# Output projection and layer norm of the first cross and first self attention in one block, the norm in two halves of tokens

## The chip, the cores and the metric

One core of one Trainium2 chip runs the whole kernel. Its engines are TensorE (PE; the load of its stationary operand is shown as PEld), VectorE (DVE), ScalarE (ACT), GpSimd (POOL) and SyncE (SP, which here issues the DMAs). Each has its own stream of instructions, and they meet only at semaphores. The metric is the device time of one launch in microseconds, before as the median of 3 runs.

## The reference, cut to what matters

A Perceiver of two layers. x is 512 rows (2 batches of 256) of 256 numbers in float32, the context 2 x 4096 rows of 256. `ln` is the layer norm without gain or bias.

```python
x = x + xattn0(ctx, ln(x), mask) @ Wo.T     # first cross attention, 16 heads of 16
x = x + sn(selfattn0(ln(x)), W_proj)        # first self attention, causal, spectral norm: a scale on the product
x = x + experts(ln(x))                      # 12 experts, the best 3 of each token, two layers and a GELU
x = x + xattn1(ln(x), ctx)                  # second cross attention, 16 heads of 64
x = x + selfattn1(ln(x)) @ Wo
x = x + quantised_ffn(ln(x))

def ln(x):
    m, v = mean(x, -1), var(x, -1)
    return (x - m) / sqrt(v + 1e-5)
```

The change concerns the ends of the first two lines (product with the output weights, addition into x) and the `ln` at the start of the second and the third.

## The kernel before, in words

The program is a row of blocks. A block holds one stream for each engine, written out by hand, with all waits between engines as counts on semaphores (`wait_ge`, `then_inc`). No scheduler moves anything. At the end of a block all engines meet before the next begins; in the trace such a border shows as a branch (L106, L1261, L1481, ...) and a stretch in which all of them idle.

x lies in SBUF as 4 tiles of 128 tokens (`NT` = 4), with 256 columns, which as the inner dimension of a product are 2 slices of 128 (`KT` = 2). PSUM has eight banks of 512 float32 columns: `banks[0:4]` are a_all and o_all, `s_banks` the four of s_all.

Place 1 lies between the first cross attention and the first self attention, place 2 between the first self attention and the experts. At both stand two blocks:

- `rows_project` (L1249). TensorE turns the attention's output with 8 transposes, slice by slice (L1282: all four tiles of slice 0 into one bank, then of slice 1). ScalarE copies each bank to `srcT` (L1297). TensorE waits for both copies and multiplies with the output weights, tile by tile, into one bank each (L1288). VectorE adds each tile into x as it comes ready, at place 1 by `add_to_x` (L1313), at place 2 with the spectral scale (L2379).
- `layer_norm` (L96). VectorE takes the statistics of four tiles (L115), aggregates them to mean and variance (L118) and adds epsilon (L120). GpSimd raises 128x4 numbers to the power -1/2 (L134). VectorE normalises four tiles into xn (L123). TensorE turns xn with 8 transposes (L146). VectorE copies slice 0 to xnT (L129), ScalarE slice 1 (L155).

Behind place 1 `self_attention` (L1441) begins. Its SyncE stream loads the weights of the experts, GpSimd splits the first half of them into two float16 parts (`halve`, L1793 and L1796) and only then turns to the causal selections (L1503) that the products with the values wait for. Behind place 2 `experts` (L1804) begins: two small products for the routing (L1846, L1850), then 144 matmuls for each layer (L1865), while VectorE compares and weighs.

`rows_project` and `layer_norm` are also used for the second cross and self attention, which the change leaves as they are.

Of the kernel before, what the change touches and what calls it, by code (L numbers as in the profile page):

```python
# [10 lines left out]
F32 = mybir.dt.float32  # L11
# [3 lines left out]
ALU = mybir.AluOpType  # L15
ACT = mybir.ActivationFunctionType
# [22 lines left out]
class Chip:  # L39


    def __init__(self, nc, ctx):
        self.nc, self.ctx, self.sems = nc, ctx, []
        self.sem_scope = ctx.enter_context(ExitStack())
        self.s_all = self.psum("s_all", 2048)
        self.s_ps = [self.s_all[:, 0:1024], self.s_all[:, 1024:2048]]
        self.s_banks = [self.s_all[:, i * 512:(i + 1) * 512] for i in range(4)]
        self.a_all, self.o_all = self.psum("a_all", 1024), self.psum("o_all", 1024)
        self.a_ps = [self.a_all[:, 0:512], self.a_all[:, 512:1024]]
        self.o_ps = [self.o_all[:, 0:512], self.o_all[:, 512:1024]]  # L50
        self.banks = [self.a_ps[0][:, :], self.a_ps[1][:, :], self.o_ps[0][:, :], self.o_ps[1][:, :],
                      *self.s_banks]
        self.x = self.sb("x", [P, NT, D], F32)
        self.xn = self.sb("xn", [P, NT, D], F32)
        self.xnT = self.sb("xnT", [P, KT, TOK], F32)
        self.ident = self.sb("ident", [P, P], F32)
        self.ones = self.sb("ones", [P, P], F32)
        self.half = self.sb("half", [P, 8], F32)
# [1187 lines left out]
                output((PAIRS - 1, W - 1))  # L1246


def rows_project(chip, tag, src, dims, weight, finish, bias_in=None, after=()):  # L1249


# [59 lines left out]
def add_to_x(chip):  # L1311
    def finish(dve, t, done):
        dve.tensor_tensor(chip.x[:, t, :], chip.banks[t][:, 0:D], chip.x[:, t, :], ALU.add).then_inc(done, 1)  # L1313
    return finish
# [1025 lines left out]
def perceiver(nc, t, out):  # L2340

    with ExitStack() as ctx:
# [17 lines left out]
        with ExitStack() as block0:  # L2360
            wo = Prefetch(chip, "o0", block0, t["a0o"])
            weights = [Prefetch(chip, f"s0{n}", block0, t[f"s0{n}"]) for n in "qkv"]
            with ExitStack() as scope:
                att = chip.sb("att0", [P, NT, D], F32, scope)
                with ExitStack() as inner:
                    buffers = SmallCrossBuffers(chip, "x0", inner, queries[0], *scratch[0])
                    cross_attention_small(chip, "x0", buffers, att, mask_out, t["ones2"], t["qrows"], t["fold"], after=[wo, *weights])
                rows_project(chip, "o0", att, D, wo, add_to_x(chip))


            layer_norm(chip, "ln1")
            with ExitStack() as scope:
                expert_weights = ExpertWeights(chip, scope, t["f0w1"], t["f0w2"], t["f0p"], t["f0u"], t["f0b"])
                att = chip.sb("att1", [P, NT, D], F32, scope)
                wo = Prefetch(chip, "o1", scope, t["s0p"])
                self_attention(chip, "s0", weights, att, [expert_weights, wo], scale=sc[:, 0:1], mask=t["causal"])

                def finish(dve, n, done):
                    dve.scalar_tensor_tensor(out=chip.x[:, n, :], in0=chip.banks[n][:, 0:D], scalar=sc[:, 1:2],  # L2379
                                             in1=chip.x[:, n, :], op0=ALU.mult, op1=ALU.add).then_inc(done, 1)  # L2380
                rows_project(chip, "o1", att, D, wo, finish)


                layer_norm(chip, "ln2")
                experts(chip, "moe", expert_weights)
        chip.recycle_semaphores()

# [96 lines left out]
```

## Time and profile before

| | |
|---|---|
| median of 3 runs | 1714.96 us |
| lowest, highest | 1714.06, 1715.53 us |
| the profiled execution | 1716.51 us |
| its span, first to last instruction | 1714.8 us |
| mean granted TensorE clock in it | 0.946 of full |
| busy TensorE, VectorE, ScalarE, GpSimd | 91%, 65%, 52%, 40% |

The profile is one execution. In its rows a name such as `o_srcT<-s_all` is the output, then the inputs; numbers in names are left out, so that `ln_st` is the tile of each layer norm and `o_pw` the weights of each output projection. `128x256 f32` are partitions and elements in each. A row of the timeline that has x4 holds four instructions merged, from the start of the first to the end of the last. The bracket at its end is the idle time of the engine before it and what ended that. PEclk is the granted TensorE clock as a share of 2.4 GHz: 1.00 is 2.4 GHz, 0.50 is 1.2 GHz.

### The profile page before, as it was taken

What the parts mean: (1) busy time and instruction counts of PE and PEld (TensorE: products, weight loads), DVE (VectorE), ACT (ScalarE), POOL (GpSimd) and SP (SyncE); (2) the same over time, 40 slices, a digit from 0 to 9 for tenths busy, and PEclk for the clock granted to TensorE, in tenths of its full rate; (3) what the DMA queues carried; (4) which work ended last, traced back from release to release, by engine and by line L of the source; (5) the groups of instructions that cost most, each with busy time, mean ns of one, the idle gap of its engine ahead of it and who ended that gap; (6) DMA issues with size and microseconds to landing.
All of it is one profiled execution on the core that took longest, in us unless ns stands there. A gap on an engine that the chain in (4) does not pass through costs nothing. (4 is left out here: it accounts for less than half of the span.)

```text
span 1714.8 us, 42108 instructions
## 1 busy us (share of the span) xinstructions
PE 1555.2 (91%) x15980; PEld 879.7 (51%) x15980; DVE 1107.0 (65%) x1786; ACT 889.4 (52%) x1204; POOL 690.9 (40%) x536
## 2 busy tenths in 40 slices
PE   7999999999499999999778958999999999996774
PEld 3455454444133333433454426777777777772442
DVE  4656656665599999996327756666666666605446
ACT  5555555554078888887241015555555555532525
POOL 5320000000111111111143108999999999951800
PEclk9999999999589999999798979999999999998887
DMA  7987978887432222220400057555556545212000
GB/s 252 225 238 207 232 233 203 232 222 182 127 95 68 67 67 67 67 67 26 157 2 1 1 141 223 151 159 142 139 153 159 156 126 162 61 35 93 2 1 13
DMA packets 178223, 212.24 MB, mean 124 GB/s; under 512 B 57096, under 2 KB 151572, under 8 KB 173486
## 3 DMA queue, kind: packets, MB, share of 16 engines
q1 hardware_dynamic: 177520, 210.44, 44.9%
q8 instruction: 93, 1.52, 0.4%
q14 instruction: 34, 0.28, 0.1%
q10 hardware_dynamic: 576, 0.00, 0.0%
HBM read 122.78 MB, written 87.57 MB: 123 GB/s over the span
## 5 line engine op out<-in xcount | busy, mean ns | idle before, releaser
L1202 POOL TENSOR_TENSOR x_r<-x_p 128x1024 f16<-128x1024 f32 x256 | 479.0, 1893 | 24.3 <-ACT x_p L1178 17.2
L1217 DVE TENSOR_REDUCE x_mx<-a_all 128x2 f32<-128x1024 f32 x249 | 304.7, 1224 | 147.2 <-PE a_all L1101 147.2
L1178 ACT ACTIVATE x_p<-s_all 128x1024 f32<-128x1024 f32 x256 | 248.4, 1022 | 223.5 <-PE s_all L1084 223.5
L769 ACT ACTIVATE x_p<-s_all 128x1024 f32<-128x1024 f32 x256 | 261.5, 1024 | 60.8 <-PE s_all L676 55.4
L824 DVE TENSOR_REDUCE x_mx<-a_all 128x1 f32<-128x512 f32 x352 | 231.5, 681 | 21.7 <-PE o_all L687 12.9
L1084 PE MATMUL s_all<-x_q,x_k 64*128 64x256 f16 x3072 | 210.2, 269 | 0.0
L1119 PEld LDWEIGHTS o_all<-x_v,x_p 128*128 128x128 bf16 x2048 | 178.7, 97 | 40.1 <-issue 40.1
L1119 PE MATMUL o_all<-x_v,x_p 128*128 128x129 f16 x2048 | 197.3, 221 | 0.9 <-POOL x_r L1202 0.9
L1120 PE MATMUL o_all<-x_v,x_r 128*128 128x65 f16 x2048 | 192.5, 193 | 0.0
L1084 PEld LDWEIGHTS s_all<-x_q,x_k 64*128 64x128 f16 x3072 | 149.5, 94 | 62.0 <-issue 0.8
L1120 PEld LDWEIGHTS o_all<-x_v,x_r 128*128 128x128 f16 x2048 | 180.7, 98 | 0.0
L715 PE MATMUL o_all<-x_p,x_vf 128*32 128x256 f32 x2048 | 163.7, 393 | 3.1 <-ACT x_osb L758 2.7
L687 PE MATMUL a_all<-x_k,x_qa 64*128 64x512 f16 x352 | 113.3, 399 | 23.3 <-DMA x_v<-values 21.8
L798 POOL TENSOR_TENSOR x_mcol<-x_nm,x_zero 128x4 f16<-128x4 f32 x32 | 6.8, 213 | 298.7 <-DVE x_nm L831 298.7
L824 DVE TENSOR_REDUCE x_mx<-o_all 128x1 f32<-128x512 f32 x160 | 109.1, 682 | 6.6 <-PE a_all L687 2.4
L1101 PE MATMUL a_all<-x_k,x_q 64*128 64x512 f16 x498 | 97.2, 387 | 12.3 <-DVE x_mx L1217 7.3
L676 PE MATMUL s_all<-x_qb,x_k 64*128 64x256 f16 x1024 | 103.9, 278 | 0.0
L233 POOL TENSOR_TENSOR q_rs<-q_ve,half 128x4 f32<-128x4 f32 x1 | 1.0, 1021 | 247.0 <-DVE q_ve L246 247.0
L1078 PE MATMUL s_all<-x_qm,x_ones 64*128 64x512 f16 x512 | 100.0, 387 | 0.0
L495 DVE TENSOR_TENSOR vst<-a_all,vst 128x512 f16<-128x512 f32 (+1 forms) x96 | 57.8, 602 | 42.1 <-ACT vst L459 41.4
L495 DVE TENSOR_TENSOR vst<-o_all,vst 128x512 f16<-128x512 f32 (+1 forms) x96 | 57.7, 602 | 41.5 <-ACT vst L459 41.0
L459 ACT ACTIVATE vst<-a_all 128x512 f16<-128x512 f32 (+1 forms) x96 | 51.5, 536 | 52.7 <-PE a_all L422 52.2
(363 smaller groups left out, 2767.7 us busy)
## 6 DMA issues: line engine op xcount, KB each, us to landing
values<-vst SPq DMA_DIRECT2D x16, 2064.0 KB, 10.5
x_v<-values SPq DMA_DIRECT2D x32, 1032.0 KB, 5.3
keys<-kst SPq DMA_DIRECT2D x32, 1024.0 KB, 6.8
x_k<-keys SPq DMA_DIRECT2D x128, 256.0 KB, 5.3
x_k<-keys SPq DMA_DIRECT2D x192, 64.0 KB, 2.1
values<-vst SPq DMA_DIRECT2D x16, 528.0 KB, 11.6
x_v<-values SPq DMA_DIRECT2D x32, 264.0 KB, 2.7
cf<-in_ctxT SPq DMA_DIRECT2D x16, 512.0 KB, 9.9
```

The source lines that it names most:

```text
L495: dve.tensor_tensor(lo, src, hi, ALU.subtract).then_inc(lo_done, 1)
L676: last = pe.matmul(chip.s_ps[g % 2][:, c * SQ:(c + 1) * SQ], kbuf[w][r, (2 * g + j) * P:(2 * g + j + 1) * P], qb[w][r, :], start=True, sto ...
L687: pe.matmul(bank(place)[:], qa[w][r, qt * P:(qt + 1) * P], kbuf[w][r, c * 512:(c + 1) * 512], start=True, stop=True).then_inc(chunk_ready, 1)
L715: last = pe.matmul(o[32 * c:32 * c + 32, 0:SQ], vf[w][:, kt, :], prob[g % NP][:, c, :], start=(g == 0), stop=(g == GR - 1), skip_group_che ...
L769: act.activation(prob[g % NP][:], chip.s_ps[g % 2][:].rearrange("p (c q) -> p c q", q=SQ), ACT.Exp, scale=hd ** -0.5).then_inc(p_ready, 1)
L824: dve.tensor_reduce(mx[a[1] % 2][:, n // 8, n % 8:n % 8 + 1], bank(place)[:], AX.X, ALU.max).then_inc(chunk_done, 1)
L1084: last = pe.matmul(s[:, c * SQ:(c + 1) * SQ], k[w][kp][r, (2 * g + j) * P:(2 * g + j + 1) * P], q[w][qp][r, :], start=False, stop=(kp == 1 ...
L1119: pe.matmul(o[:, qt * VC:(qt + 1) * VC], hi, v[w][:, kt, :], start=begin, stop=False, skip_group_check=True)
L1120: last = pe.matmul(o[:, qt * VC:qt * VC + 1 + hd], rest[i][:, c, qs], v[w][:, kt, 0:1 + hd], start=False, stop=end, skip_group_check=True)
L1178: act.activation(prob[g % NP][:], chip.s_ps[g % 2][:].rearrange("p (c q) -> p c q", q=SQ), ACT.Exp, scale=hd ** -0.5).then_inc(p_ready, 1)
L1202: pool.tensor_tensor(rest[g % NP][:], prob[g % NP][:], hi, ALU.subtract).then_inc(rest_done, 1)
L1217: dve.tensor_reduce(mx[a[1] % 2][:, n // 4, 2 * (n % 4):2 * (n % 4) + 2], chunk_banks(u, g)[:, :].rearrange("p (h c) -> p h c", h=2), AX.X ...
```

## The change

At both places the two blocks become one, `project_and_norm`, and `layer_norm` is no longer called there. The transposes of the attention's output are ordered by halves of tokens, tiles 0 and 1 in one bank and tiles 2 and 3 in the other, and the product of a tile waits only for the copy of its half. VectorE takes the statistics of a tile directly behind its addition; a class `HalfNorm` then does variance, power, normalisation, transposes and copy for tiles 0 and 1 and for tiles 2 and 3. The transposes of xn go to `s_banks[2:4]`, and ScalarE copies both halves.

```diff
--- before.py
+++ after.py
@@ -1244,6 +1244,106 @@
 
                 all_units(body)
                 output((PAIRS - 1, W - 1))
+
+class HalfNorm:
+
+    def __init__(self, chip, tag, scope, banks):
+        self.chip, self.banks = chip, banks
+        self.st = chip.sb(f"{tag}_st", [P, NT, 6], F32, scope)
+        self.mv = chip.sb(f"{tag}_mv", [P, NT, 2], F32, scope)
+        self.ve = chip.sb(f"{tag}_ve", [P, NT], F32, scope)
+        self.rs = chip.sb(f"{tag}_rs", [P, NT], F32, scope)
+        (self.stats, self.spread, self.var, self.rstd, self.normed, self.turned, self.copied) = (
+            chip.sem(f"{tag}_{n}") for n in ("stats", "aggr", "var", "rstd", "xn", "tr", "trout"))
+
+    def stats_of(self, dve, t, src):
+        dve.bn_stats(self.st[:, t, :], src).then_inc(self.stats, 1)
+
+    def variance(self, dve, h):
+        dve.wait_ge(self.stats, 2 * h + 2)
+        for t in (2 * h, 2 * h + 1):
+            dve.bn_aggr(self.mv[:, t, :], self.st[:, t, :]).then_inc(self.spread, 1)
+        dve.wait_ge(self.spread, 2 * h + 2)
+        hs = slice(2 * h, 2 * h + 2)
+        dve.tensor_scalar(self.ve[:, hs], self.mv[:, hs, 1], 1e-5, None, ALU.add).then_inc(self.var, 1)
+
+    def power(self, pool, h):
+        hs = slice(2 * h, 2 * h + 2)
+        pool.wait_ge(self.var, h + 1)
+        pool.tensor_tensor(self.rs[:, hs], self.ve[:, hs], self.chip.half[:, hs], ALU.pow).then_inc(self.rstd, 1)
+
+    def apply(self, dve, t, out, src):
+        dve.wait_ge(self.rstd, t // 2 + 1)
+        dve.tensor_scalar(out, src, self.mv[:, t, 0:1], self.rs[:, t:t + 1], ALU.subtract, ALU.mult).then_inc(self.normed, 1)
+
+    def turn(self, pe, h):
+        pe.wait_ge(self.normed, 2 * h + 2)
+        for k in range(KT):
+            for t in range(2):
+                last = pe.transpose(self.banks[h][:, (2 * k + t) * P:(2 * k + t + 1) * P],
+                                    self.chip.xn[:, 2 * h + t, k * P:(k + 1) * P], self.chip.ident[:])
+        last.then_inc(self.turned, 1)
+
+    def copy(self, act, h):
+        act.wait_ge(self.turned, h + 1)
+        act.activation(self.chip.xnT[:, :, h * 2 * P:(h + 1) * 2 * P], self.banks[h].rearrange("p (k t) -> p k t", k=KT),
+                       ACT.Copy).then_inc(self.copied, 1)
+
+def project_and_norm(chip, tag, src, weight, finish):
+
+    nc = chip.nc
+    with ExitStack() as scope:
+        w = weight.w
+        srcT = chip.sb(f"{tag}_srcT", [P, KT, TOK], F32, scope)
+        norm = HalfNorm(chip, f"{tag}_ln", scope, chip.s_banks[2:4])
+        tr, tr_out, ready, done = (chip.sem(f"{tag}_{n}") for n in ("tr", "trout", "rdy", "done"))
+        with nc.Block() as block:
+            @block.gpsimd
+            def _(pool):
+                for h in range(2):
+                    norm.power(pool, h)
+
+            @block.tensor
+            def _(pe):
+                for h in range(2):
+                    for k in range(KT):
+                        for t in range(2):
+                            last = pe.transpose(chip.s_banks[h][:, (2 * k + t) * P:(2 * k + t + 1) * P],
+                                                src[:, 2 * h + t, k * P:(k + 1) * P], chip.ident[:])
+                    last.then_inc(tr, 1)
+                pe.wait_ge(weight.loaded, 16)
+                for t in range(NT):
+                    pe.wait_ge(tr_out, t // 2 + 1)
+                    for k in range(KT):
+                        last = pe.matmul(chip.banks[t][:, 0:D], srcT[:, k, t * P:(t + 1) * P], w[:, k, :],
+                                         start=(k == 0), stop=(k == KT - 1))
+                    last.then_inc(ready, 1)
+                for h in range(2):
+                    norm.turn(pe, h)
+
+            @block.scalar
+            def _(act):
+                for h in range(2):
+                    act.wait_ge(tr, h + 1)
+                    act.activation(srcT[:, :, h * 2 * P:(h + 1) * 2 * P], chip.s_banks[h].rearrange("p (k t) -> p k t", k=KT),
+                                   ACT.Copy).then_inc(tr_out, 1)
+                for h in range(2):
+                    norm.copy(act, h)
+
+            @block.vector
+            def _(dve):
+                for h in range(2):
+                    for t in (2 * h, 2 * h + 1):
+                        dve.wait_ge(ready, t + 1)
+                        finish(dve, t, done)
+                        dve.wait_ge(done, t + 1)
+                        norm.stats_of(dve, t, chip.x[:, t, :])
+                    norm.variance(dve, h)
+                for t in range(NT):
+                    norm.apply(dve, t, chip.xn[:, t, :], chip.x[:, t, :])
 
 def rows_project(chip, tag, src, dims, weight, finish, bias_in=None, after=()):
@@ -2365,10 +2465,8 @@
                 with ExitStack() as inner:
                     buffers = SmallCrossBuffers(chip, "x0", inner, queries[0], *scratch[0])
                     cross_attention_small(chip, "x0", buffers, att, mask_out, t["ones2"], t["qrows"], t["fold"], after=[wo, *weights])
-                rows_project(chip, "o0", att, D, wo, add_to_x(chip))
-
-
-            layer_norm(chip, "ln1")
+                project_and_norm(chip, "o0", att, wo, add_to_x(chip))
+
             with ExitStack() as scope:
                 expert_weights = ExpertWeights(chip, scope, t["f0w1"], t["f0w2"], t["f0p"], t["f0u"], t["f0b"])
                 att = chip.sb("att1", [P, NT, D], F32, scope)
@@ -2378,10 +2476,7 @@
                 def finish(dve, n, done):
                     dve.scalar_tensor_tensor(out=chip.x[:, n, :], in0=chip.banks[n][:, 0:D], scalar=sc[:, 1:2],
                                              in1=chip.x[:, n, :], op0=ALU.mult, op1=ALU.add).then_inc(done, 1)
-                rows_project(chip, "o1", att, D, wo, finish)
-
-
-                layer_norm(chip, "ln2")
+                project_and_norm(chip, "o1", att, wo, finish)
                 experts(chip, "moe", expert_weights)
         chip.recycle_semaphores()
```

VectorE's stream at place 1, from the last branch ahead of it to the first behind it; `o0` is this projection, `ln1` the norm behind it. Before:

```order
L1303 UNCONDITIONAL_BRANCH
L1313 TENSOR_TENSOR x<-a_all,x 128x256 x2
L1313 TENSOR_TENSOR x<-o_all,x 128x256 x2
L1261 UNCONDITIONAL_BRANCH
L112 UNCONDITIONAL_BRANCH
L115 BN_STATS ln1_st<-x 128x6 x4
L118 BN_AGGR ln1_mv<-ln1_st 128x2 x4
L120 TENSOR_SCALAR ln1_ve<-ln1_mv 128x4
L123 TENSOR_SCALAR xn<-x,ln1_mv,ln1_rs 128x256 x4
L129 COPY xnT<-a_all 128x512
L106 UNCONDITIONAL_BRANCH
```

And of the changed kernel:

```order
L1336 UNCONDITIONAL_BRANCH
L1413 TENSOR_TENSOR x<-a_all,x 128x256
L1262 BN_STATS o0_ln_st<-x 128x6
L1413 TENSOR_TENSOR x<-a_all,x 128x256
L1262 BN_STATS o0_ln_st<-x 128x6
L1267 BN_AGGR o0_ln_mv<-o0_ln_st 128x2 x2
L1270 TENSOR_SCALAR o0_ln_ve<-o0_ln_mv 128x2
L1413 TENSOR_TENSOR x<-o_all,x 128x256
L1262 BN_STATS o0_ln_st<-x 128x6
L1413 TENSOR_TENSOR x<-o_all,x 128x256
L1262 BN_STATS o0_ln_st<-x 128x6
L1267 BN_AGGR o0_ln_mv<-o0_ln_st 128x2 x2
L1270 TENSOR_SCALAR o0_ln_ve<-o0_ln_mv 128x2
L1279 TENSOR_SCALAR xn<-x,o0_ln_mv,o0_ln_rs 128x256 x4
L1303 UNCONDITIONAL_BRANCH
```

The statistics have moved in between the additions, variances and epsilon come once for each two tiles, all normalisations still stand in a row behind the second variance, and the copy to xnT is gone.

TensorE's stream at place 1, `att0` being the attention's output. Before:

```order
L1276 UNCONDITIONAL_BRANCH
L1282 MATMUL s_all<-ident,att0 128x128 x8
L1288 MATMUL a_all<-o0_pw,o0_srcT 128x256 x4
L1288 MATMUL o_all<-o0_pw,o0_srcT 128x256 x4
L1261 UNCONDITIONAL_BRANCH
L139 UNCONDITIONAL_BRANCH
L146 MATMUL a_all<-ident,xn 128x128 x8
L106 UNCONDITIONAL_BRANCH
```

And of the changed kernel:

```order
L1309 UNCONDITIONAL_BRANCH
L1314 MATMUL s_all<-ident,att0 128x128 x8
L1321 MATMUL a_all<-o0_pw,o0_srcT 128x256 x4
L1321 MATMUL o_all<-o0_pw,o0_srcT 128x256 x4
L1285 MATMUL s_all<-ident,xn 128x128 x8
L1303 UNCONDITIONAL_BRANCH
```

The transposes of xn follow the products without a branch, into s_all. The place 2 has the same rows with `o1`, `att1` and `ln2`.

## Rows read from the trace of the kernel before

**Rows 1.** Timeline, place 1: start, duration, engine, line, operation, tiles, count, [idle before].
```profile
815.37 1.38 PE L1282 MATMUL s_all<-ident,att 128*128 128x128 f32 x8 [0.97 <-PEq L649]
816.04 0.60 ACT L1297 ACTIVATE o_srcT<-s_all 128x512 f32<-128x512 f32 x1 [2.38 <-PE s_all L1282]
816.79 0.60 ACT L1297 ACTIVATE o_srcT<-s_all 128x512 f32<-128x512 f32 x1 [0.15 <-PE s_all L1282]
...
819.61 0.42 DVE L1313 TENSOR_TENSOR x<-a_all,x 128x256 f32<-128x256 f32 x1 [4.78 <-PE a_all L1288]
...
823.00 0.42 DVE L1313 TENSOR_TENSOR x<-o_all,x 128x256 f32<-128x256 f32 x1 [1.26 <-PE o_all L1288]
823.87 0.42 DVE L1313 TENSOR_TENSOR x<-o_all,x 128x256 f32<-128x256 f32 x1 [0.44 <-PE o_all L1288]
824.82 1.40 DVE L115 BATCH_NORM_STATS2 ln_st<-x 128x6 f32<-128x256 f32 x4 [0.53 <-PEq L1261]
826.25 0.38 DVE L118 BATCH_NORM_AGGREGATE ln_mv<-ln_st 128x2 f32<-128x6 f32 x4
826.67 0.17 DVE L120 TENSOR_SCALAR ln_ve<-ln_mv 128x4 f32<-128x4 f32 x1
826.92 1.02 POOL L134 TENSOR_TENSOR ln_rs<-ln_ve,half 128x4 f32<-128x4 f32 x1 [26.70 <-DVE ln_ve L120]
827.97 1.38 DVE L123 TENSOR_SCALAR xn<-x,ln_mv,ln_rs 128x256 f32<-128x256 f32 x4 [1.13 <-POOL ln_rs L134]
...
829.41 1.97 PE L146 MATMUL a_all<-ident,xn 128*128 128x128 f32 x8 [5.58 <-DVE xn L123]
830.56 0.69 DVE L129 COPY xnT<-a_all 128x512 f32<-128x512 f32 x1 [1.21 <-PE a_all L146]
831.41 0.60 ACT L155 ACTIVATE xnT<-a_all 128x512 f32<-128x512 f32 x1 [14.03 <-PE a_all L146]
```

**Rows 2.** Timeline, place 2.
```profile
893.64 1.08 ACT L1297 ACTIVATE o_srcT<-s_all 128x512 f32<-128x512 f32 x2 [2.54 <-PE s_all L1282]
...
896.01 0.48 DVE L2379 SCALAR_TENSOR_TENSOR x<-a_all,sn,x 128x256 f32<-128x256 f32 x1 [3.57 <-PE a_all L1288]
...
898.60 0.48 DVE L2379 SCALAR_TENSOR_TENSOR x<-o_all,sn,x 128x256 f32<-128x256 f32 x1 [0.38 <-PE o_all L1288]
...
906.20 0.60 ACT L155 ACTIVATE xnT<-a_all 128x512 f32<-128x512 f32 x1 [11.47 <-PE a_all L146]
```

**Rows 3.** Groups by line and form, 811 to 834: busy us, mean ns of one.
```profile
L115 DVE BATCH_NORM_STATS2 ln_st<-x 128x6 f32<-128x256 f32 x4 | 1.4, 414 | 0.5 <-PEq L1261 0.5
L123 DVE TENSOR_SCALAR xn<-x,ln_mv,ln_rs 128x256 f32<-128x256 f32 x4 | 1.4, 407 | 1.1 <-POOL ln_rs L134 1.1
```

**Rows 4.** Stretches: length, busy PE, PEld, DVE, ACT, POOL, PEclk, DMA, GB/s.
```profile
816.00:822.80 6.80, 6.02 (x18) 4.58 (x16) 0.85 (x2) 1.19 (x2) 0.00 (x0) 0.50 0.00 0
826.20:839.80 13.60, 7.20 (x14) 3.52 (x15) 3.63 (x15) 1.40 (x3) 2.58 (x3) 0.50 0.47 165
901.20:918.30 17.10, 12.48 (x32) 5.90 (x33) 8.57 (x44) 2.66 (x5) 1.01 (x1) 0.50 0.00 1
```

**Rows 5.** Timeline, GpSimd's first selection in the first self attention.
```profile
869.34 1.24 POOL L1503 TENSOR_SCALAR_AFFINE_SELECT s_p<-s_p 128x512 f32<-128x512 f32 x2 [0.32 <-ACT s_p L1702]
```

**Rows 6.** The page's groups: a small tensor-tensor of GpSimd.
```profile
L798 POOL TENSOR_TENSOR x_mcol<-x_nm,x_zero 128x4 f16<-128x4 f32 x32 | 6.8, 213 | 298.7 <-DVE x_nm L831 298.7
```

**Rows 7.** Timeline, VectorE's casts and GpSimd's memset behind place 1.
```profile
832.28 0.52 POOL L1494 MEMSET s_nm<- 128x512 f16 x1 [4.34 <-POOLq L106]
...
832.32 0.56 DVE L1709 CAST s_ident<-ident 128x128 f16<-128x128 f32 x1 [1.07 <-PEq L106]
...
834.06 0.23 DVE L1713 CAST s_mkb<-ident 128x128 bf16<-128x128 f32 x1 [1.11 <-DMA s_mk<-in_causal]
```

**Rows 8.** Timeline, expert matmuls at both clocks.
```profile
917.95 0.60 PE L1865 MATMUL s_all<-ewh,moe_xl 128*128 128x512 f16 x1
...
918.38 0.39 PE L1865 MATMUL s_all<-ewh,moe_xh 128*128 128x512 f16 x1
```

## The prediction

> **What bounds the kernel now.** I read four views, in this order. The busy shares of the whole span (the table of the section on the profile) have TensorE at 91%. That says nothing of the two places the change touches, because there the engines work one after another. The timeline of the first place [rows 1] shows it as a chain: each instruction starts when one on another engine ends. Follow it down: transposes, a ScalarE copy, projection matmuls, VectorE's adds, the statistics, GpSimd's power, VectorE's normalisation, transposes, a copy. No other work of the program lies beside it, so whatever is taken out of this chain comes off the time. The second place [rows 2] is the same chain at the doubled clock. The table of stretches [rows 4] then shows at which clock TensorE ran there, and the timeline of the stage behind [rows 5] what could swallow a gain.
>
> Call E the end of the last of the four adds into x. At place 1, E is 823.87 + 0.42 = 824.29, and the last copy into xnT ends at 831.41 + 0.60 = 832.01: 7.72 us [rows 1]. At place 2, E is 898.60 + 0.48 = 899.08 and the copy ends at 906.20 + 0.60 = 906.80: again 7.72 us [rows 2]. The two blocks together are all that the change edits.
>
> **From E to the end of the norm, per place** [rows 1, 3].
> - The block border. Before, the statistics start at 824.82, 0.53 after E. Now a wait on the same engine stands there; the nearest row is from the end of the statistics (826.22) to the aggregation (826.25), 0.03. Gain 0.50.
> - Statistics. Four in 1.40 before. Now three are done while TensorE projects, and one, 0.41 [rows 3], stands behind E. Gain 0.99.
> - Aggregation: two of four behind E, half of 0.38. Gain 0.19. The addition of epsilon stays (0.17).
> - The power on GpSimd. Its input has two columns where it had four. No row shows that. It costs at most the 1.02 of four columns; the cheapest tensor-tensor of GpSimd with this shape, another operation, takes 0.21 [rows 6]. I take 1.02, the row of the same operation. If it is 0.21, the normalisations of half 0 (0.73) hide it, and 0.45 more is gained at each place.
> - Normalisation. Half 0 is normalised while GpSimd works on half 1. On VectorE's stream, variance(1) stands ahead of apply(0), so half 0 isn't early; it only fills the wait. Behind the power two of four are left: 0.41 + 0.32 = 0.73 in place of 1.38 (0.32 is the step from one to the next, (1.38 - 0.41)/3). Gain 0.65.
> - Transposes and copy. Before, ScalarE's copy waited for all eight, 829.41 to 831.41, 2.00. Now half 1 has four; the row for four at this clock is the start of VectorE's copy, 830.56 - 829.41 = 1.15. Gain 0.85. The copy is ScalarE's in both (0.60); of the split form I know no row, so 0.60 to the 0.69 of VectorE's copy. VectorE's copy, now ScalarE's, lay beside the transposes before, and copy(0) lies there now: 0.
>
> Sum: 0.50 + 0.99 + 0.19 + 0.65 + 0.85 = 3.18 us per place, 6.36 for two.
>
> **Ahead of E.** The projection of tiles 0 and 1 no longer waits for the second ScalarE copy, only for the first.
> - Place 1: the copies start at 816.04 and 816.79, so matmuls start 0.75 earlier, soon after 816.64. TensorE is free by then, give or take a tenth: its transposes end at 816.75. VectorE keeps up, since at the low clock a tile comes each 1.7 us (from the first add to the third, 3.39 for two) and its add, its statistics and two waits take 0.9. Tile 2's add moves from 823.00 to 822.25. Tile 3 ran mostly behind the rise of the clock at 822.8 [rows 4], and this rise I leave where it is. From tile 2's add on, 0.55 us at the low clock does what 0.275 does at the high one, and of the 0.87 that a tile takes at the high clock (823.00 to 823.87) 0.595 is left behind 822.80: tile 3's add starts at 823.40. So E moves from 824.29 to 823.82: gain 0.47, bounds 0 and 0.75.
> - Place 2: one copy is 0.54 [rows 2], so tile 0's add starts at 895.47. But tiles come every 0.86 (four adds, 896.01 to 898.60) and VectorE now needs 0.48 + 0.03 + 0.41 = 0.92 for each, plus 0.42 for aggregation and epsilon of half 0. From 895.47: three rounds of 0.92 and 0.42 give 898.65, the fourth add ends at 899.13, against 899.08. Gain 0; bounds 0 and 0.54. What hid the statistics at place 1, the slow matmuls, isn't there.
>
> Total 6.36 + 0.47 + 0 = 6.83 us.
>
> **What it meets behind.** The loads of the expert weights are issued in the self-attention block behind place 1, and GpSimd splits them ahead of its first selection. They move with the start of that block, so the 3.65 us of place 1 are not lost to them. GpSimd has only 0.32 us of idle time before that selection [rows 5], though: a further gain on TensorE there (a clock that rises sooner) would run into GpSimd. Behind place 2 the expert block starts on xnT and everything in it is issued relative to that. All else of the program, before and behind, keeps its instructions.
>
> The profiled execution took 1716.51, 1.55 above the median of the runs, 1714.96; its span was 1714.8. 1716.51 - 6.83 = 1709.7 for such an execution, and for the median 1714.96 - 6.83 = 1708.1.
>
> **A rule that speaks against it.** The new overlap, normalisation of half 0 on VectorE beside the power on GpSimd, is one that before never had: GpSimd idled during all of VectorE's part and the reverse [rows 1]. In this kernel VectorE and GpSimd can disturb each other. A cast of 128x128 takes 0.56 beside GpSimd's memset and 0.23 alone [rows 7]. The Trainium skill, SBUF — State Buffer, "Who interferes with whom", says why: the two engines share a pair of ports that one instruction holds whole, when VectorE's runs in a two-port mode, and it lists copy, cast and tensor_scalar among those that can. The normalisation is a tensor_scalar. For it speaks only its kind; against it, that it takes 0.41 for 256 elements [rows 3] where the undisturbed cast takes 0.23 for 128, nearly in proportion, so no mode shows as faster than the other. That doesn't decide it.
>
> **Rivals.**
> 1. Port. One of the two waits for the other. If power(1) waits for both normalisations, it starts 0.73 - 0.05 = 0.68 later; if they wait for it, four stand behind it again, 0.65. Either way 0.7 per place: 6.83 - 1.4 = 5.4, time 1709.5. Chance 0.08.
> 2. The clock holds. TensorE's granted clock is at 1.2 GHz (0.50 of full) from 826.2 to 839.8 and from 901.2 to 918.3 [rows 4]; both falls come in the idle stretch between last projection and first transposes of xn (5.6 us at place 1 [rows 1]). The change cuts that stretch to about 2 us, with transposes of half 0 in it. If the clock stayed up, the eight transposes save about 0.5 per place (four took 815.37 to 816.04, 0.67, at the high clock and 1.15 at the low one), 1.0 in all. In the expert block at most half of TensorE's 12.48 busy us goes, 6.2; but VectorE's routing and first weighings lie in the same stretch, 8.57 us busy, and TensorE may be only four tiles ahead of them, so I take 4 of the 6.2. At place 1 rows 5 let little through, about 1. Together 6.83 + 1.0 + 4 + 1 = 12.8, time about 1702. Against it: even the split stretch is over half idle. The Trainium skill, TensorE: Matmul & The Clock Gate, "The HAM clock gate", says that the low clock is the default that activity lifts; by that too a shorter idle stretch is the better one, but rows give no bound. Chance 0.12, mostly for a part of it.
> 3. No change that can be told. What the borders and waits cost comes back: the power of half 1 queued behind, added waits, a rise of the clock that comes later. It needs 3.4 of the 6.83 lost. Chance 0.06.
> 4. Slower. The mechanism is a clock that stays low for long behind place 2: expert matmuls start every 0.43 at 1.2 GHz [rows 8] and so every 0.215 at 2.4. To lose 6.83 and 3.43 more, 10.3/0.215 = 48 further matmuls must run low; with all 144 of the first layer low it is 31 us at most, and the time at most 1708.1 + 31 = 1739. Against it: before, the rise came at 918.3 once they were issued without a gap. Chance 0.03.
>
> **How the numbers follow.** The forecast as summed has 0.71. Its own spread: power and transposes up to 0.9 each on the good side, the clock's rise in the next block about 1 us either way, copies and waits 0.5 on the bad one: 1705.3 to 1710. With the port and part of the clock's luck the range is 1705 to 1711. A measurement of this kernel can tell about 0.2%, 3.4 us, from no change; that is a time of 1711.5. Faster: 0.71 + 0.12 + 0.08 = 0.91, less 0.01 for mixed mishaps: 0.90. Same 0.07, slower 0.03.
>
> **What would show it.** From E to the end of the last xnT copy: 4.5 us at both places, for 7.72. The last add of place 2 no earlier than before, of place 1 about half a us earlier, counted from the first transpose. A two-column power near 1.0. Normalisations 0 and 1 beside the power, at 0.41 each; longer ones, or a power that starts late, would be the port. GpSimd's first selection at the same distance from the start of the self-attention block. The forecast is wrong if these hold and the total doesn't move, or if the granted clock's low stretches differ by several us.

## The result, and the profile after

Six runs of each kernel on one chip: 1709.20 us (1706.46 to 1710.82) for 1714.51 (1713.23 to 1717.57). The ratio is 0.9966, 95% interval 0.9953 to 0.9979: 3.6 to 8.1 us off, forecast 6.8. Later I measured the changed kernel twice more, each time beside before on one chip: 0.9938 (0.9925 to 0.9950) and 0.9949 (0.9930 to 0.9967). The three ratios are worth 5.8, 10.6 and 8.8 us; the first was the smallest, and I estimate the true gain at 8 to 10 us. That the kernel is faster is shown by all three. Its size is less certain: the intervals of the first and the second comparison don't overlap, and no run shows why.

The profiled execution took 1710.64, with a span of 1708.9. Place 1 in its timeline; columns as in [rows 1], which these rows answer.

```profile
818.28 1.06 PE L1314 MATMUL s_all<-ident,att 128*128 128x128 f32 x8 [0.97 <-PEq L649]
818.94 1.09 ACT L1331 ACTIVATE o_srcT<-s_all 128x512 f32<-128x512 f32 x2 [2.39 <-PE s_all L1314]
...
819.68 1.96 PE L1321 MATMUL a_all<-o_pw,o_srcT 128*128 128x256 f32 x8 [0.34 <-ACT o_srcT L1331]
820.83 0.42 DVE L1413 TENSOR_TENSOR x<-a_all,x 128x256 f32<-128x256 f32 x1 [3.09 <-PE a_all L1321]
...
821.28 0.43 DVE L1262 BATCH_NORM_STATS2 o_ln_st<-x 128x6 f32<-128x256 f32 x1
...
823.76 0.41 DVE L1413 TENSOR_TENSOR x<-o_all,x 128x256 f32<-128x256 f32 x1
824.21 0.43 DVE L1262 BATCH_NORM_STATS2 o_ln_st<-x 128x6 f32<-128x256 f32 x1
824.67 0.25 DVE L1267 BATCH_NORM_AGGREGATE o_ln_mv<-o_ln_st 128x2 f32<-128x6 f32 x2
824.95 0.17 DVE L1270 TENSOR_SCALAR o_ln_ve<-o_ln_mv 128x2 f32<-128x2 f32 x1
825.03 0.73 DVE L1279 TENSOR_SCALAR xn<-x,o_ln_mv,o_ln_rs 128x256 f32<-128x256 f32 x2
825.20 0.79 POOL L1275 TENSOR_TENSOR o_ln_rs<-o_ln_ve,half 128x2 f32<-128x2 f32 x1 [1.35 <-DVE o_ln_ve L1270]
...
825.81 0.66 PE L1285 MATMUL s_all<-ident,xn 128*128 128x128 f32 x4 [2.43 <-DVE xn L1279]
826.02 0.73 DVE L1279 TENSOR_SCALAR xn<-x,o_ln_mv,o_ln_rs 128x256 f32<-128x256 f32 x2 [0.27 <-POOL o_ln_rs L1275]
...
826.82 0.88 PE L1285 MATMUL s_all<-ident,xn 128*128 128x128 f32 x4 [0.35 <-DVE xn L1279]
827.73 0.60 ACT L1291 ACTIVATE xnT<-s_all 128x512 f32<-128x512 f32 x1 [0.63 <-PE s_all L1285]
```

E is 823.76 + 0.41 = 824.17, the last copy ends at 828.33: 4.16 us for 7.72. One statistics instruction stands behind E where four stood, and the second pair of normalisations starts 0.03 behind the power. Place 2, for [rows 2]:

```profile
895.89 0.47 DVE L2477 SCALAR_TENSOR_TENSOR x<-o_all,sn,x 128x256 f32<-128x256 f32 x1
...
900.16 0.60 ACT L1291 ACTIVATE xnT<-s_all 128x512 f32<-128x512 f32 x1 [0.87 <-PE s_all L1285]
```

4.40 us, again for 7.72. The stretches by clock, for [rows 4]: length, busy time of PE, PEld, DVE, ACT, POOL, granted clock, DMA share, GB/s.

```profile
816.00:820.00 4.00, 2.09 (x18) 1.70 (x15) 0.36 (x2) 1.44 (x3) 0.00 (x0) 1.00 0.00 0
820.00:827.10 7.10, 4.32 (x23) 3.34 (x22) 5.39 (x18) 0.62 (x2) 1.50 (x2) 1.00 0.01 2
827.10:837.40 10.30, 6.28 (x12) 2.49 (x11) 0.72 (x4) 1.40 (x4) 1.45 (x2) 0.50 0.75 282
898.80:912.40 13.60, 11.77 (x29) 5.11 (x30) 6.40 (x35) 3.15 (x6) 0.00 (x0) 0.50 0.00 0
```

Call the front the time from the last write of the first attention's output to E. At place 1 the clock is now at 2.4 GHz through all products. In before it fell at 816.0, and the front took 9.46 us; here it took 6.43. Against that stands a loss: behind xnT the first projection waits longer.

The table cuts all fourteen profiles at the same points, from their timelines. Its rows are named after the experiments of the next section. A: last write of the first attention's output. E: end of the last addition into x. C: end of the last copy to xnT. P: first projection of the self attention. B: last write of its output. L: first product of the experts. "Fall" is when the granted clock fell between A and E, counted from A, and "low" is how long it then stayed at 1.2 GHz.

```
us              A-E1  fall  low   E1-C1  C1-P   P-B    B-E2  E2-C2  C2-L  L-end
before          9.46  +1.2  6.8   7.72   2.56   57.87  6.64  7.72   0.30  807.67
before again    8.27  +2.8  3.4   7.73   2.65   57.62  6.64  7.71   0.31  807.29
after           6.43  none    -   4.16   3.39   58.02  6.62  4.40   0.30  807.85
after again     6.44  none    -   3.93   3.18   56.85  6.61  4.40   0.30  806.55
after third     6.44  none    -   3.93   3.23   56.72  6.62  3.94   0.31  806.89
place 1 only    6.44  none    -   3.93   2.94   56.91  6.64  7.73   0.30  806.62
place 2 only    8.27  +2.7  3.4   7.74   2.61   57.55  6.61  4.40   0.30  807.23
held            7.67  +0.8  3.4   4.78   2.94   58.17  6.62  5.14   0.31  807.17
merged whole    7.39  +1.2  3.4   7.46   2.96   57.16  6.16  7.45   0.30  807.81
early products  6.09  none    -   7.74   2.61   57.00  6.16  7.71   0.31  807.16
late products   9.45  +1.2  6.8   4.40   4.28   57.05  7.11  3.94   0.30  806.72
spare block     8.53  +2.5  3.4   3.94   2.56   57.58  6.62  4.39   0.31  807.25
mask early      6.44  none    -   3.93   1.42   57.77  6.62  4.39   0.30  807.43
loads early     7.66  +0.6  3.4   3.94   1.42   57.62  6.62  4.40   0.30  807.23
```

A itself lies between 814.2 and 817.9 in them, in code that is the same in all. This scatter of nearly 4 us is larger than most terms of the sum, which is why what follows goes by segments and not by times.

### The profile page after: what moved, and what is told of

The parts are those of the page before. It is cut to its first block and busy times, and to the rows that moved or that the text cites. A ratio compares the mean times of both kernels' runs of the same rounds, so it can differ in the third digit from the quotient of the medians.

```text
span 1708.9 us, 42088 instructions
## 1 busy us (share of the span) xinstructions
PE 1553.2 (91%) x15980; PEld 877.4 (51%) x15980; DVE 1106.8 (65%) x1786; ACT 891.3 (52%) x1206; POOL 692.9 (41%) x538
## 5 line engine op out<-in xcount | busy, mean ns | idle before, releaser
L1202 POOL TENSOR_TENSOR x_r<-x_p 128x1024 f16<-128x1024 f32 x256 | 479.3, 1895 | 23.9 <-ACT x_p L1178 17.1
```

What stands on the lines that cost most here:

```text
L1202: pool.tensor_tensor(rest[g % NP][:], prob[g % NP][:], hi, ALU.subtract).then_inc(rest_done, 1)
```

## The experiments

**The kernel before, again**, unedited.

> The kernel before, once more, for a second profile. Segments between fixed points of the timeline: from the end of the first cross attention (last write of att) to E (last addition into x) 9.46 us in the first profile, E to the end of xnT 7.72, from there to the first projection of the self attention 2.56, place 2: 6.64, 7.72, 0.30. Theory (fixed lengths, only TensorE's clock differs between executions): 7.72 and 7.72 again within 0.2; the 9.46 is 6.6 where the clock is at 2.4 GHz there, 9.5 where it falls to 1.2 as in the first profile. Rival (before always has the low clock at place 1, and the change lifts it): 9.46 again.

1717.82 us, one run. E to C is 7.73 and 7.71: these lengths repeat. The front was 8.27, with the clock falling at 820.7:

```profile
818.41 1.06 PE L1282 MATMUL s_all<-ident,att 128*128 128x128 f32 x8 [0.97 <-PEq L649]
819.08 1.08 ACT L1297 ACTIVATE o_srcT<-s_all 128x512 f32<-128x512 f32 x2 [2.38 <-PE s_all L1282]
...
820.30 3.36 PE L1288 MATMUL a_all<-o_pw,o_srcT 128*128 128x256 f32 x8 [0.83 <-ACT o_srcT L1297]
```

TensorE stood idle for 0.83 us ahead of the products, and 0.4 us after they began the clock fell; most of them ran at 1.2 GHz (the row has 3.36 us where after has 1.96).

**The changed kernel, again**, unedited.

> The changed kernel once more, with a profile and five rounds. First profile: end of attention to E 6.43, E to xnT 4.16 at place 1 and 4.40 at place 2, xnT to the first projection 3.39 (the causal mask landed 2.6 us after its issue; 1.8 in before). Theory of the sum: E to xnT 4.1 to 4.6 at both places, time 5 to 8 us under before, ratio about 0.9960. Rival clock: 6.43 is luck, in this profile it can be 9.0 (low clock). Rival mask: the earlier block makes the mask land late every time, 3.4 again; if it is scatter of the transfer, 2.6 to 3.4.

Ratio 0.9938 (0.9925 to 0.9950). Front 6.44 and no fall, for the second time. The causal mask, which the first projection waits for, was late again (C1-P 3.18). Luck alone became less likely for either.

**Place 1 only**

```diff
-                project_and_norm(chip, "o1", att, wo, finish)
+                rows_project(chip, "o1", att, D, wo, finish)
+                layer_norm(chip, "ln2")
```

> The change at place 1 only (output projection of the first cross attention and the norm behind it); place 2 as before. Theory of the sum: 3.2 us from E to xnT, 0 to 0.75 ahead of E by clock, so 3.2 to 3.9 us under before; place 2 at 6.64 + 7.72. Rival (the gain of place 1 is taken back by the wait for the mask or by GpSimd's split of the expert weights in the block behind): under 2.5 us, with the segment from xnT to the end of the self attention longer by the difference.

Ratio 0.9968 (0.9956 to 0.9980), 3.4 to 7.5 us off. E to C 3.79 less than before, and the front again without a fall. The gain isn't taken back.

**Place 2 only**, the same edit at place 1.

> The change at place 2 only (output projection of the first self attention and the norm behind it); place 1 as before. Theory of the sum: 3.2 to 3.4 us under before, all of it between E and xnT (7.72 to 4.4), nothing ahead of E (6.6 in both). Rival (the low clock of the expert block grows by what the norm shrinks): under 2 us, with a longer segment behind xnT.

Ratio 0.9975 (0.9965 to 0.9986), 2.4 to 6.0 us off. All of it lies in E2-C2, 4.40 for 7.72; the front at place 2 is 6.61 for 6.64. The low clock in the experts took nothing back: L-end is 807.23 for 807.67 and 807.29.

**Held normalisations**

```diff
+                dve.wait_ge(norm.rstd, 2)
                 for t in range(NT):
                     norm.apply(dve, t, chip.xn[:, t, :], chip.x[:, t, :])
```

> The changed kernel, but all four normalisations of a place wait for the power of half 1. It takes away the overlap of VectorE's normalisation with GpSimd's power. Theory of the sum: E to xnT grows by 0.65 to 0.75 at each place, from about 4.0 and 4.4 to 4.7 and 5.1; the second power stays at 0.8 or falls to 0.70. Rival port (the two engines block one another in the changed kernel): nearly no growth, since two normalisations beside the power would cost what four behind it do, and the second power falls clearly.

Ratio 0.9949 (0.9929 to 0.9968). E1-C1 is 4.78, against 3.93 to 4.16, and E2-C2 grew from 4.40 to 5.14, by 0.74. Its rows at place 2:

```profile
897.19 0.70 POOL L1275 TENSOR_TENSOR o_ln_rs<-o_ln_ve,half 128x2 f32<-128x2 f32 x1 [1.47 <-DVE o_ln_ve L1270]
897.93 1.38 DVE L1279 TENSOR_SCALAR xn<-x,o_ln_mv,o_ln_rs 128x256 f32<-128x256 f32 x4 [0.81 <-POOL o_ln_rs L1275]
```

The normalisations end 3.14 behind E where after has 2.59: the overlap is worth 0.55, which is the 0.65 of the sum less the 0.1 by which the power is slower beside it. The other 0.19 lies behind them: here all eight transposes stand there in a row, while in after those of half 0 are out of the way by then. So 0.74 comes near to 0.65 by two deviations that cancel in part.

The second power takes 0.70 alone and 0.79 to 0.80 beside the two normalisations (0.79 in the rows of after), in all profiles that have this overlap. So the two engines do disturb each other, by 0.1 us. The normalisation keeps its 0.41. The rival as I stated it, one waiting for the other's whole work, is refuted.

**Merged, norm whole**: the block of after, and behind E the stream of before.

```diff
-                    for t in (2 * h, 2 * h + 1):
-                        ...
-                        norm.stats_of(dve, t, chip.x[:, t, :])
-                    norm.variance(dve, h)
+                for t in range(NT):
+                    dve.wait_ge(ready, t + 1)
+                    finish(dve, t, done)
+                dve.wait_ge(done, NT)
+                for t in range(NT):
+                    norm.stats_of(dve, t, chip.x[:, t, :])
+                ...    # aggregation, epsilon, power, normalisation, transposes, copies as in layer_norm
```

> The changed kernel with early products and one block, but behind E the norm is done whole as before: four statistics, four aggregations, one power of four columns, four normalisations, eight transposes, two copies. Only the block border is gone. Theory of the sum: E to xnT 7.72 - 0.50 = 7.2 at both places; 3 us each above the changed kernel. Rival (the merged block itself is most of the gain): below 6.5.

Ratio 0.9985 (0.9973 to 0.9996). E to C is 7.46 and 7.45, not 7.2.

```profile
821.67 0.42 DVE L1423 TENSOR_TENSOR x<-o_all,x 128x256 f32<-128x256 f32 x1 [0.44 <-PE o_all L1321]
822.13 1.41 DVE L1262 BATCH_NORM_STATS2 o_ln_st<-x 128x6 f32<-128x256 f32 x4
823.57 0.38 DVE L1349 BATCH_NORM_AGGREGATE o_ln_mv<-o_ln_st 128x2 f32<-128x6 f32 x4
824.05 0.17 DVE L1351 TENSOR_SCALAR o_ln_ve<-o_ln_mv 128x4 f32<-128x4 f32 x1
824.37 1.02 POOL L1307 TENSOR_TENSOR o_ln_rs<-o_ln_ve,half 128x4 f32<-128x4 f32 x1 [24.29 <-DVE o_ln_ve L1351]
825.50 1.38 DVE L1279 TENSOR_SCALAR xn<-x,o_ln_mv,o_ln_rs 128x256 f32<-128x256 f32 x4 [1.28 <-POOL o_ln_rs L1307]
```

The border's term is as summed: 0.04 from E (822.09) to the statistics for 0.53 in before. Three hand-overs behind it are 0.06 to 0.08 longer each than in [rows 1], to epsilon 0.10, to the power 0.15, back 0.11. What makes them longer in this kernel stays open. Merging alone is a small part of the gain; the halves are the larger.

**Early products**: the two blocks of before, with the order of the transposes and the waits of the products as in after.

```diff
+                if split:    # the tags "o0" and "o1"
+                    ...      # transposes: tiles 0 and 1, then 2 and 3, one bank each
                 for t in range(NT):
+                    if split:
+                        pe.wait_ge(tr_out, t // 2 + 1)
```

> The kernel before with only the transposes of the attention's output ordered by halves and the products of a half released by its own copy, both blocks kept. As predicted: end of attention to E 0.47 shorter at a low clock; place 2 6.64 - 0.54 = 6.1 (no statistics in VectorE's way). Theory clock (the shorter gap between transposes and products at place 1, 0.3 for 0.8 us, keeps TensorE at 2.4 GHz): 6.0 at place 1 with a granted clock of 1.00 up to the last product, where the three profiles without early products had 8.3 to 9.5 and those with them 6.4. Rival luck (the clock's fall there has nothing to do with the order): 7.5 or more.

Ratio 0.9982 (0.9970 to 0.9995). Front 6.09, clock at 1.00 from 814.0 to 824.4:

```profile
814.00:824.40 10.40, 5.12 (x28) 4.07 (x27) 4.02 (x15) 1.08 (x2) 0.87 (x1) 1.00 0.00 0
```

At place 2 the front is 6.16 for 6.64, 0.48 shorter, where the sum has 0.54 for one copy.

**Late products**

```diff
+                pe.wait_ge(tr_out, 2)
                 for t in range(NT):
-                    pe.wait_ge(tr_out, t // 2 + 1)
```

> The changed kernel with the products waiting for both copies again. Theory clock: the clock falls at place 1 between transposes and products as in before, end of attention to E 8.3 to 9.5, time 2 to 3 us above the changed kernel. Theory of the sum as predicted: 0.5 to 0.75 more at place 1, and at place 2 about 0.3 to 0.5 more. Rival luck: 6.4 + 0.5 = 6.9 to 7.2 at a clock of 1.00.

Ratio 0.9957 (0.9945 to 0.9970). Front 9.45, and place 2 7.11 for 6.62. The fall came at +1.2, ahead of the first product in either version, so the order of the products didn't cause it. Merged whole, with early products, has its fall at +1.2 too, and the two differ in what follows. Late products, the low stretch and the products of tiles 0 and 1:

```profile
815.40:822.20 6.80, 6.02 (x17) 4.57 (x16) 2.12 (x7) 1.19 (x2) 0.10 (x1) 0.50 0.00 0
816.86 3.75 PE L1321 MATMUL a_all<-o_pw,o_srcT 128*128 128x256 f32 x8 [0.78 <-ACT o_srcT L1331]
```

And merged whole:

```profile
815.86:819.25 3.39, 3.35 (x11) 2.54 (x9) 0.42 (x1) 1.19 (x2) 0.00 (x0) 0.50 0.02 5
819.30:826.00 6.70, 2.33 (x11) 1.72 (x9) 3.73 (x14) 0.00 (x0) 1.02 (x1) 1.00 0.00 0
816.65 3.26 PE L1321 MATMUL a_all<-o_pw,o_srcT 128*128 128x256 f32 x8
```

With late products TensorE idled for 0.78 us ahead of them and the clock stayed low for 6.8 us; with early ones no idle time is shown there, and it rose after 3.4. The fronts are 9.45 and 7.39. Merged whole has no statistics between its additions, which is worth 0.34 without a fall (6.43 for 6.09); held and loads early have them, fell at +0.8 and +0.6, rose after 3.4 us as well, and took 7.67 and 7.66. Before stands with late products: +1.2, 6.8, 9.46. So the five profiles with an early fall divide by the order of the products.

The other falls divide nearly so. Products start at A + 1.9 with early products at the high clock, and at A + 2.4 (at the high clock) to 2.7 without. Falls at +0.6 to +1.2 are in both kinds (before, held, merged whole, late products, loads early), and when they come looks like luck. Falls at +2.5 to +2.8 are in three profiles, two without early products and the spare block, whose extra border moves its products to A + 2.4. In none of the nine others with early products did the clock fall after +1.2 ahead of E. With so few profiles that is likely rather than shown; the difference after an early fall rests on two profiles against three.

**Spare block** ahead of `project_and_norm` at place 1.

```diff
+                with chip.nc.Block() as block:
+                    @block.vector
+                    def _(dve):
+                        dve.tensor_copy(chip.ones[:, 0:1], chip.half[:, 0:1])
                 project_and_norm(chip, "o0", att, wo, add_to_x(chip))
```

> The changed kernel with a spare block (one copy of one column on VectorE) ahead of the projection of place 1. It moves all that follows in the program by one block, as the layer norm's block did in before. In the four profiles with two blocks a transfer of instructions of queue 14 lies 3 us ahead of the end of xnT and the mask lands 1.8 to 1.9 us after its issue; in the six with one block it lies 1.2 to 1.7 us behind it, right ahead of the mask's landing, at 2.2 us or more. Theory (the place of that instruction transfer delays the mask): if the spare block moves the transfer, first projection 2.6 us behind xnT again. Rival (the mask is late for another reason): 2.9 or more with the transfer elsewhere.

Ratio 0.9956 (0.9942 to 0.9970). C1-P fell to 2.56. In after, the mask's issue, VectorE's casts behind its landing, and the transfers by queue and kind from 829 to 832 (packets, MB, share of 16 engines) are:

```profile
828.59 0.36 SPq L1585 DMA_DIRECT2D s_mk<-in_causal  x1
...
831.21 0.23 DVE L1813 CAST s_mkb<-ident 128x128 bf16<-128x128 f32 x1 [2.21 <-DMA s_mk<-in_causal]
...
831.72 3.75 PE L1614 MATMUL o_all<-xnT,s0q_pw 128*128 128x512 f32 x4 [4.02 <-DVE s_mkb L1814]
```

```profile
q1 hardware_dynamic: 186, 0.58, 73.2%
q14 instruction: 1, 0.01, 0.7%
```

And with the spare block, from 830 to 833 (q14 had its transfer at 819.5):

```profile
830.19 0.36 SPq L1585 DMA_DIRECT2D s_mk<-in_causal  x1
...
831.98 0.23 DVE L1813 CAST s_mkb<-ident 128x128 bf16<-128x128 f32 x1 [1.11 <-DMA s_mk<-in_causal]
```

```profile
q1 hardware_dynamic: 168, 0.36, 52.8%
```

With the transfer of instructions out of the way the cast started 1.79 us behind the issue, with it 2.62 us. Twelve profiles load the mask in this block. In seven of them such a transfer comes 1.2 to 1.7 us behind C, and C1-P is 2.94 to 4.28. In the other five, the spare block's among them, it comes 2.9 us or more ahead of C, and C1-P is 2.56 to 2.65. That the transfer and the late mask go together is shown; through what it delays the mask is not.

**Mask early**: its load issued in the projection block of place 1, and no longer in the self-attention block.

```diff
+            @block.sync
+            def _(sp):
+                for p in early:
+                    p.loads(sp)
...
-                project_and_norm(chip, "o0", att, wo, add_to_x(chip))
+                rows = MaskRows(chip, scope, t["causal"])
+                project_and_norm(chip, "o0", att, wo, add_to_x(chip), early=[rows])
```

> The changed kernel with the causal mask's load issued in the projection block of place 1, about 10 us ahead of the self-attention block that uses it. Theory mask (in the merged kernels the first projection waits 2.9 to 3.4 us, once 4.3, behind xnT for the mask; 2.6 in before): the first projection starts about 1.2 us behind xnT. But GpSimd's first selection stays 36.9 us or more behind xnT, since GpSimd first splits the expert weights, whose load keeps its place; it was 36.9 to 38.3, so 0 to 1.4 us are gained in all. Rival (the projections wait for something else): 2.6 us or more remain.

1706.26 us, ratio 0.9937 (0.9916 to 0.9958). C1-P 1.42. GpSimd now came to its first selection straight from the split:

```profile
858.09 6.00 POOL L1921 TENSOR_TENSOR ewl<-ew,ewh 128x3072 f16<-128x3072 f32 x1
864.04 1.24 POOL L1607 TENSOR_SCALAR_AFFINE_SELECT s_p<-s_p 128x512 f32<-128x512 f32 x2
```

No idle time stands ahead of the selection. It came 36.1 us behind C, a little under the 36.9 that I had as the floor. The issue of the weights no longer stands behind the mask's in SyncE's stream, and came 0.25 behind C for 0.67 in after; how much of the 0.8 that explains is open.

**Loads early**: `early=[rows, expert_weights]`.

> As the kernel with the early mask, and the loads of the expert weights issued there too, 10 us earlier. Theory: GpSimd is done with the split before the first selection is due, so the selection comes 34.5 to 36.2 us behind xnT (1.2 and the 33.7 to 34.9 from first projection to selection), 1.5 to 2.5 us under the changed kernel. Rival (nothing in that block waits for GpSimd): no difference to the kernel with the early mask.

1707.81 us, ratio 0.9949 (0.9930 to 0.9969). GpSimd idled 9.96 us ahead of the selection:

```profile
848.79 6.02 POOL L1921 TENSOR_TENSOR ewl<-ew,ewh 128x3072 f16<-128x3072 f32 x1
864.76 1.24 POOL L1607 TENSOR_SCALAR_AFFINE_SELECT s_p<-s_p 128x512 f32<-128x512 f32 x2 [9.96 <-ACT s_p L1807]
```

but C to B was 59.04 for the 59.19 of the early mask. The rival held: freeing GpSimd gave nothing that can be told. The clock rose 4.7 us behind P here and 5.0 with the early mask, and half of that difference is the 0.15.

GpSimd held up the end of this block in none of the fourteen profiles. P-B less half the time from P to the clock's rise is 55.2 to 55.3 in every one of them. Early products is the plainest: there the first of ScalarE's two instructions ended 0.8 us ahead of the selection that uses it, because GpSimd was still splitting, and P-B is 57.00 with the rise 3.4 behind P:

```profile
863.96 1.69 ACT L1717 ACTIVATE s_p<-s_all,s_s 128x1024 f32<-128x1024 f32 x2 [0.95 <-PE s_all L1597]
859.90 6.00 POOL L1811 TENSOR_TENSOR ewl<-ew,ewh 128x3072 f16<-128x3072 f32 x1
865.85 1.24 POOL L1518 TENSOR_SCALAR_AFFINE_SELECT s_p<-s_p 128x512 f32<-128x512 f32 x2
```

**The changed kernel, a third time**, beside those two.

> The changed kernel a third time, beside the two with early loads. End of attention to E 6.4 where the clock holds at place 1 and 7.4 to 8.3 where it falls (the kernel that waits with the normalisations fell to 7.67 with the same front); E to xnT 3.9 to 4.6 and 4.4; mask again behind 2.2 us of transfer.

1706.61 us, ratio 0.9949 (0.9930 to 0.9967). C to B was 59.95, so the early mask saves 0.8 us there, and 0.9 with the early loads, for 1.8 less from C to P. The reason that only half is left is the clock. It rose 6.1 us behind C in this run and with the early loads alike, so what starts 1.8 us sooner does so at 1.2 GHz. The times can't tell the three apart. No version that clearly beats the changed kernel was found.

## Why the prediction was right, point by point

- **E to xnT, 3.18 per place**: right, a little undersized: 3.56 and 3.32 in the first profile. The power was mis-sized, 0.79 where I took 1.02, inside its bounds. At place 1 the transposes of half 1 add as much: 0.91 from their start to the copy for 1.15, since the clock fell only while they ran (allowed for as 0.5 on the good side). The border was confirmed (0.49 for 0.50). The overlap gave 0.55 for 0.65, because the power beside it is 0.1 slower.
- **Place 2 ahead of E, 0**: right, for the reason given. Early products alone give 0.48, and VectorE's statistics take it: 6.16 with whole statistics behind E, 6.62 with them in between. They would have cost time with late products (7.11).
- **Place 1 ahead of E, 0.47 with bounds 0 and 0.75**: this step failed. I wrote of the clock's rise "this rise I leave where it is", and left its fall in place too, both as one profile had them. All three profiles of the changed kernel have 6.43 to 6.44 for 9.46 and 8.27, so 1.8 to 3.0. The change doesn't only start the products sooner at whatever clock there is. Falls behind A + 2.5 no longer came, and where the clock fell early it rose after 3.4 us instead of 6.8. That none of the three had an early fall, as three other kernels with early products did (fronts of 7.39 to 7.67), is luck.
- **Behind place 1, nothing**: wrong by 0.5 to 0.8. The mask lands later, and C-P is 3.2 to 3.4 for 2.6. I read the self-attention block's start as moving rigidly with xnT, and checked the loads for their issue, not for what else moves on the DMA queues. At the end of the block the loss is less: C to B is 60.14 with the spare block, and 59.95, 60.03 and 61.41 in the changed kernel, where the clock's rise weighs more than the mask.
- **GpSimd's cap on a sooner rise**: not there. P-B goes with the time the clock stays low behind P, 58.02 where it rises 5.6 us behind P and 56.72 where it is 2.9. That is half of each us, in runs where GpSimd idled 9.96 us ahead of its selection and in runs where it came up to 0.8 late. The 0.32 of idle time in rows 5 was no bound on the block.
- **The clock's low stretches**: I named a difference of several us in them as a sign that the forecast is wrong, and it came. The clock still fell behind both places, but behind place 2 it stayed low for 17.1 us in before and 13.7, 6.8 and 3.4 in the changed kernel. Before again has 10.2, so much of this is scatter. Little of it reached the time: L-end is 807.67 and 807.29 before, and 806.55 to 807.85 changed, so the 4 us of rival 2 were far too much.
- **Total**: from A to L before has 92.3 and 90.9, the changed kernel 83.3, 81.7 and 81.2. The means differ by 9.5, for 6.83 forecast: 2.0 more ahead of E at place 1, 0.8 more from E to xnT in both places together, 0.7 lost at the mask, 0.5 gained in P-B by the clock. The first comparison, 5.3 between its medians, lay below this by scatter that stays unexplained. So the forecast of 6.83 came close to it partly by luck: the undersized front, the missed mask and that scatter partly cancel.

## What to carry to other kernels

Where engines hand one result from one to the next, working in halves pays by what the second half leaves behind the last wait; sum that tail instruction by instruction, and it comes out to a few tenths. Give the clock its own term wherever the change shortens an idle stretch of TensorE, also a short one of under 1 us: ask both whether it falls there and how soon it rises again, and take more than one profile of before. An engine with no idle time ahead of an instruction is not yet the bound; free it, as the early loads did, and see. And look at what a block loads for itself at its start: a load of 1.8 us that all engines wait for is exposed, and moving it one block ahead took 1.8 us off the wait, of which half was left at the end of the block, because the clock rose no sooner.

## What the runs showed of the hardware

- The power on GpSimd takes 1.02 us for four columns and 0.70 for two; beside VectorE's normalisation 0.79 to 0.80. The Trainium skill, SBUF — State Buffer, "Who interferes with whom", has an instruction of VectorE in a two-port mode block GpSimd for its whole length. Here the delay is 0.1 where the two normalisations last 0.73; whether they ran in such a mode, no run shows.
- With the clock's fall 1.2 us behind A in both, its low stretch lasted 6.8 us with late products and 3.4 us with early ones.
- While the clock is low behind place 1, the self-attention block loses half of that time: P-B is 58.02 with 5.6 us from P to the rise and 56.72 with 2.9.
- One transfer of 0.01 MB of instructions goes with the cast behind a small load starting 0.3 to 1.7 us later.
- Adding or removing one block moves such transfers by microseconds: 1.7 us behind C in after, 10.5 ahead of it with the spare block, 3.0 ahead in before.
